# A fused window-attention block and separable convolution, its strips of rows worked one by one or in pairs

## The chip, the cores and the metric

One core of one Trainium2 chip runs the kernel as one program. Its engines are TensorE (PE, matmuls; PEld is its weight load), VectorE (DVE), ScalarE (ACT), GpSimd (POOL) and SyncE (SP), which only issues DMAs here. Each runs its own list of instructions in order, and they meet at semaphores. The metric is device time in microseconds (us).

## The reference, cut to what matters

The input x is (16, 112, 112, 96) in float32. First comes a block of shifted-window attention, then a depthwise 3 x 3 convolution with a pointwise one and a batch norm:

```python
xn = layer_norm(x); xs = roll(xn, (-3, -3)); windows of 7 x 7 tokens
q, k, v = windows @ qkv_w + qkv_b          # 3 heads of 32
attn = softmax(q k^T * scale + bias + mask)  # 49 x 49 per window and head
x1 = x + roll(window_reverse(attn v @ proj_w + proj_b), (3, 3))
y  = x1 + fc2(gelu(fc1(layer_norm(x1))))     # 96 -> 384 -> 96
z  = depthwise_3x3(relu(y)) + dw_bias
out = batch_norm(z @ pw_kernel + pw_bias)
```

## The kernel before, in words

A strip is one row of 16 windows, 7 image rows of 112 pixels. There are 16 of them per image and 256 in all. Everything is float32. Each engine has a function `step(t, phase)` that calls the stages in an order written out by hand, and `steps` calls it for every t with strips at different stages in it: in step t, strip t has its softmax and attention, t+1 its queries, keys and values, t+2 its turn of x, t+3 its first layer norm, t-1 its MLP, t-3 its depthwise convolution and t-4 its pointwise convolution and its store.

The stages, with the engine and the line of their main instruction:

- `scores` (PE, L346) multiplies queries and keys into banks 0 to 2. `add_bias` (DVE, L810) adds the bias table and writes `prob`, `find_max` (DVE, L819) takes the row maxima, `shift` (POOL, L954) subtracts them, `exps` (ACT, L573) takes exponentials, `add_up` (DVE, L826 and L828) sums and takes reciprocals, `divide` (POOL, L963) scales. Each of these is three instructions per strip, one per group of heads. `prob` exists once, so add_bias waits for the turned probabilities of the strip before.
- `turn_probs` (PE, L465) transposes `prob` after `divide`, `probs_turned` (ACT, L635) copies it out, `weigh_values` (PE, L474) multiplies with the values, `attention_out` (ACT, L648 to L653) writes `attnT`, `project` (PE, L535) follows.
- `turn_probs` of groups 0 and 1 uses the banks from which `values` (DVE, L861) copies the next strip's values, so it waits for that copy (`v_ready`).
- `add_x` (DVE, L905, L868 to L883) adds the input and takes the second layer norm's statistics; `root` (POOL, L969, L972) makes scales; `normalise` (ACT, L606) and `rest` (POOL, L980) share the seven columns of tokens, four and three. `turn_x1`, `x1_turned` (PE L411, ACT L616) turn it.
- The MLP is `hidden` (PE, L428), `gelus` (ACT, L627) and `second_layer` (PE, L442 and L446), in two halves. `into_map` (ACT, L682) writes relu of the sum into `ymap`, a ring of areas of rows.
- The depthwise convolution is nine taps over the map, `tap` 0 (DVE, L848) and `tap` 1 to 8 (DVE, L850), each one pass over 7 x 112 pixels. For the strip next to an image's last one each tap is split in two. `pointwise` (PE, L523), `outputs` (ACT, L599) and SP's `store` end a strip.
- The first layer norm is `norm_x` (DVE), `first_scale` and `first_rest` (POOL), `first_norm` (ACT); `turn_x` (PE, L509) and `x_turned` (ACT, L663) turn it; `queries_keys` and `values` follow (PE, L376, L379, L394).
- ACT needs one table for the exponential and another for Gelu. `load_gelu` (L688) and `load_exp` (L692) are one-element activations that bring the load forward. In every strip there is one of each.
- SP issues in each step `move_keys` (part of the keys to other partitions), `store` and `load` of a later strip's input.

The lists that set the order are the calls of `step` at L540 to L557 (PE), L704 to L726 (ACT), L910 to L932 (DVE) and L1002 to L1012 (POOL).

Of the kernel before, what the change touches and what calls it, by code (L numbers as in the profile page):

```python
# [58 lines left out]
AREAS = 6  # L59
TOP_ROWS, LOW_ROWS = 5, 2  # L60

ACT_NORM = HALVES[0][1]
BIAS_LOADS = NT + 1
UNROLL = 4


def swin_conv_kernel(nc, x, qkv_w, qkv_b, proj_w, proj_b, rel_bias_rt, ln1_g, ln1_b, ln2_g, ln2_b,
# [25 lines left out]
    def steps(eng, step, first=-4):  # L93

        for t in range(first, NS + 4):
            step(t, t % UNROLL)
# [13 lines left out]
    with ExitStack() as ctx:  # L110
# [28 lines left out]
        x1 = sb("x1", PT_, 2, WS, C)  # L139
# [76 lines left out]
        def _(sp):  # L216
# [20 lines left out]
            def load(t, phase):  # L237
                s = t + 4
                if not has(s):
                    return  # L240
                slot = phase

                wait(sp, x1_ready, nth(t, 2, 1))
# [8 lines left out]
            def store(t, phase):  # L252
                i = t - 4
                if not has(i):
                    return
                slot = phase % 2

                wait(sp, out_ready, nth(i, 2, 1))
                image, k = i // NWIN, (i + 1) % NWIN
# [6 lines left out]
            def move_keys(t):  # L266
                if not has(t + 1):
                    return
                for u, (a, b) in enumerate(((96, 64), (32, 0))):
                    wait(sp, q_ready, nth(t + 1, 2, u))  # L270
                    sp.dma_start(k0[b:b + HD, :], qk[a:a + HD, u * HALF:(u + 1) * HALF]).then_inc(k0_moved, 16)

            def step(t, phase):
                move_keys(t)
                store(t, phase)
                load(t, phase)

            load(-4, 0)
            load(-3, 1)
            load(-2, 2)  # L280
# [16 lines left out]
            steps(sp, step, first=-1)  # L297
            stores = [(NS + 1) // 2, NS // 2]
            sp.wait_ge(out_stored[1], 32 * stores[0])
            sp.wait_ge(out_stored[0], 32 * stores[1])  # L300
# [3 lines left out]
        def _(pe):  # L304
# [24 lines left out]
            def scores(t):  # L329
                if not has(t):  # L330
                    return
                wait(pe, q_ready, nth(t, 2, 1))
                wait(pe, k_copied, nth(t, 1, 0))
                wait(pe, k0_moved, 32 * (t + 1))
                wait(pe, o_ready, nth(t - 1, 1, 0))
                wait(pe, h_ready, nth(t - 2, 6, 5))
                if t < 2:
                    wait(pe, xt_ready, nth(t + 1, 2, 1))
# [31 lines left out]
            def queries_keys(t):  # L370
                if not has(t + 1):
                    return
# [713 lines left out]
```

## Time and profile before

| | |
|---|---|
| median of 3 runs | 5510.72 us (5488.98 to 5522.0) |
| the profiled execution's own time | 5488.53 us |
| its span, first to last instruction | 5486.8 us |
| PE busy | 5291.6 us (96%) |
| DVE busy | 5129.3 us (93%) |
| ACT busy | 5060.9 us (92%) |
| POOL busy | 3786.2 us (69%) |
| mean granted TensorE clock | 0.993 |
| loads of an ACT table | 255 at L688, 254 at L692, 1283 ns each |

Busy time is the time in which an engine had at least one instruction under way. Matmuls overlap in the engine's pipeline and their ends are modelled, so the distance from the start of one group of matmuls to the start of the next is the better measure of what a group takes. Waits for an own earlier result, on DVE above all, are in no busy sum. The time column of the timeline is us from the span's start.

### The profile page before, as it was taken

The numbers are of one execution on the slowest core, as the hardware profiler recorded it, in microseconds if no ns is written. First come the engines' busy times: TensorE is split into PE (matmuls) and PEld (weight loads), VectorE is DVE, ScalarE is ACT, GpSimd is POOL, SyncE is SP. The second block draws the span as 40 slices with busy tenths as digits, with TensorE's granted clock in tenths as the row PEclk, the third lists the DMA queues.
The fourth block names the chain that finished last, engine by engine and source line by source line (L and its number), as shares of the span: only waits on it lengthen the run. The fifth ranks groups of instructions, "written<-read, shape, count | busy, mean of one in ns | idle before, by whom it ended". The sixth has DMA issues, their size and how long they took to land.

```text
span 5486.8 us, 203158 instructions
## 1 busy us (share of the span) xinstructions
PE 5291.6 (96%) x81186; PEld 3789.4 (69%) x81186; DVE 5129.3 (93%) x13773; ACT 5060.9 (92%) x11038; POOL 3786.2 (69%) x4105
## 2 busy tenths in 40 slices
PE   5999999999999999999999999999999999999998
PEld 3767767676766676767777676767676767677675
DVE  4999999999999999999999999999999999999998
ACT  4999999999999999999999999999999989999996
POOL 3777767777777677777777677777777767777673
PEclk9999999999999999999999999999999999999998
DMA  1111111111111111111111111111111111111110
GB/s 25 34 36 35 36 36 37 35 36 35 36 35 36 35 36 35 36 35 36 36 35 38 36 36 35 36 35 36 36 36 36 37 34 36 36 35 36 37 36 24
DMA packets 275650, 193.70 MB, mean 35 GB/s; under 512 B 229160, under 2 KB 246041, under 8 KB 274713
## 3 DMA queue, kind: packets, MB, share of 16 engines
q1 hardware_dynamic: 274712, 180.70, 12.6%
q8 instruction: 650, 10.65, 0.8%
q14 instruction: 288, 2.35, 0.1%
HBM read 77.81 MB, written 77.07 MB: 28 GB/s over the span
## 4 chain that ended last, share of the span: by engine, by line
PE 57%; DVE 19%; ACT 12%; issue 6%; POOL 4%; SPq 1%; DVEq 0%; DMA 0%; ACTq 0%; POOLq 0%
PE bank L428 19%; PE bank L446 18%; DVE smax L819 7%; DVE prob L810 7%; PE bank L535 6%; PE bank L346 6%; PE bank L474 4%; ACT probT L635 4%; POOL prob L954 3%; ACT xT L663 3%; ACT o_tile L599 3%; PE bank L442 3%; DVE acc L850 2%; ACT prob L573 1%; POOL prob L963 1%
## 5 line engine op out<-in xcount | busy, mean ns | idle before, releaser
L850 DVE SCALAR_TENSOR_TENSOR acc<-ymap,taps,acc 96x784 f32<-96x784 f32 (+2 forms) x2176 | 2137.3, 987 | 54.9
L969 POOL TENSOR_TENSOR rstd<-var_eps,minus_half 112x7 f32<-112x7 f32 x512 | 1114.0, 2176 | 1266.0 <-DVE var_eps L883 1266.0
L428 PE MATMUL bank<-x1T,w 96*128 96x448 f32 (+1 forms) x3072 | 1148.3, 510 | 19.7 <-issue 10.5
L446 PE MATMUL bank<-hT,w 128*96 128x448 f32 (+1 forms) x3072 | 1097.1, 493 | 0.0
L627 ACT ACTIVATE hT<-bank,bfc 128x448 f32<-128x448 f32 (+1 forms) x1536 | 772.6, 564 | 11.9 <-PE bank L428 11.4
L428 PEld LDWEIGHTS bank<-x1T,w 96*128 96x128 f32 x3072 | 542.8, 190 | 346.6 <-issue 204.3
L954 POOL TENSOR_TENSOR prob<-prob,smax 128x392 f32<-128x392 f32 x768 | 653.6, 851 | 159.2 <-DVE smax L819 147.0
L980 POOL TENSOR_SCALAR xn<-x_in,minus_mean,rstd 112x96 f32<-112x96 f32 x768 | 680.9, 897 | 45.2 <-POOL offset L972 45.1
L446 PEld LDWEIGHTS bank<-hT,w 128*96 128x96 f32 x3072 | 466.3, 163 | 342.4 <-issue 165.4
L963 POOL TENSOR_TENSOR prob<-prob,srec 128x392 f32<-128x392 f32 x768 | 632.2, 852 | 81.7 <-DVE srec L828 81.7
L682 ACT ACTIVATE ymap<-bank,cols 96x128 f32<-96x128 f32 (+6 forms) x1056 | 603.2, 679 | 92.4 <-PE bank L446 92.4
L573 ACT ACTIVATE prob<-prob 128x392 f32<-128x392 f32 x768 | 411.6, 536 | 136.5 <-POOL prob L954 117.9
L810 DVE TENSOR_TENSOR prob<-bank,table 128x392 f32<-128x392 f32 x768 | 430.6, 561 | 104.3 <-PE bank L346 104.2
L535 PEld LDWEIGHTS bank<-wproj,attnT 97*112 97x112 f32 x3584 | 396.9, 179 | 102.4 <-issue 100.7
L819 DVE TENSOR_REDUCE smax<-prob 128x8 f32<-128x392 f32 x768 | 430.7, 561 | 26.5
L394 PEld LDWEIGHTS bank<-wv,xT 96*49 96x49 f32 x8192 | 366.4, 125 | 99.6 <-issue 99.6
L523 PE MATMUL bank<-wpw,acc 97*112 97x96 f32 x3584 | 416.4, 268 | 17.2 <-DVE acc L850 16.3
L606 ACT ACTIVATE x1n<-x,offset,rstd 112x96 f32<-112x96 f32 x1024 | 394.2, 456 | 29.6 <-POOL offset L972 10.8
L606 ACT ACTIVATE xn<-x_in,offset,rstd 112x96 f32<-112x96 f32 x1024 | 390.4, 451 | 29.4 <-POOL offset L972 29.4
L663 ACT COPY xT<-bank 96x448 f32<-96x448 f32 (+1 forms) x512 | 400.0, 887 | 16.3 <-PE bank L509 7.0
L376 PE MATMUL bank<-xT,wqk 96*128 96x392 f32 x1024 | 409.6, 523 | 1.1 <-ACT xT L663 1.0
L523 PEld LDWEIGHTS bank<-wpw,acc 97*112 97x112 f32 x3584 | 374.1, 178 | 51.2 <-DVE acc L850 17.0
(100 smaller groups left out, 10286.4 us busy)
## 6 DMA issues: line engine op xcount, KB each, us to landing
out<-o_tile SPq DMA_DIRECT2D x256, 210.0 KB, 2.5
x_in<-in_x SPq DMA_DIRECT2D x256, 168.0 KB, 2.9
x_in<-in_x SPq DMA_DIRECT2D x256, 126.0 KB, 2.9
k<-qk SPq DMA_DIRECT2D x512, 49.0 KB, 1.9
out<-o_tile SPq DMA_DIRECT2D x256, 84.0 KB, 2.5
hT<-in_L_conv_rel_bias SPq DMA_DIRECT2D x49, 0.6 KB
x1T<-in_L_conv_fc_w SPq DMA_DIRECT2D x1, 144.0 KB, 2.6
w<-in_L_conv_fc_w SPq DMA_DIRECT2D x1, 144.0 KB, 2.4
```

Source lines behind the costliest of these rows:

```text
L428: pe.matmul(bank[(1, 2, 5)[m]][:, 0:n * PT_], w1[:, m * 128:(m + 1) * 128], x1T[:, first * PT_:(first + n) * PT_], start=True, stop=True). ...
L446: mm = pe.matmul(bank[b][0:C, 0:n * PT_], w2[:, m, :], hT[:, m, first * PT_:(first + n) * PT_], start=False, stop=(m == MC - 1))
L523: mm = pe.matmul(bank[3 + i][0:HW, a * C:(a + 1) * C], acc[:, phase % 2, first + a, :], wpw[:], start=True, stop=True)
L535: mm = pe.matmul(bank[b][0:PT_, a * C:(a + 1) * C], attnT[:, col * WS:(col + 1) * WS, :], wproj[:], start=True, stop=True)
L606: last = act.activation(dst[:, j], src[:, j], ACT.Identity, bias=b["offset"][:, j:j + 1], scale=b["rstd"][:, j:j + 1])
L627: act.activation(hT[:, m, first * PT_:(first + n) * PT_], bank[(1, 2, 5)[m]][:, 0:n * PT_], ACT.Gelu_apprx_tanh, bias=bfc1[:, m:m + 1]).th ...
L810: dve.tensor_tensor(prob[:, at, 0:NT], bank[g][:, 0:PAIRS * NT].rearrange("p (a m) -> p a m", m=NT), bias[:, at], ALU.add).then_inc(s_bias ...
L819: dve.tensor_reduce(smax[:, at], prob[:, at, 0:NT], AX_X, ALU.max).then_inc(max_ready, 1)
L850: last = dve.scalar_tensor_tensor(out=dst, in0=src, scalar=taps[:, i:i + 1], in1=dst, op0=ALU.mult, op1=ALU.add)
L954: pool.tensor_tensor(p, p, m, ALU.subtract).then_inc(shifted, 1)
L963: pool.tensor_tensor(p, p, r, ALU.mult).then_inc(p_ready, 1)
L969: pool.tensor_tensor(b["rstd"][:], b["var_eps"][:], minus_half[0:PT_], ALU.pow)\
```

## The change

`steps` now goes over pairs of strips, (a, b) = (a, a + 1), and each engine's list is written for a pair. The softmax parts of a and of b come after each other in the first half, the MLPs of a-1 and of a in the second. One `load_exp` and one `load_gelu` stand in a pair's list. The banks of PSUM are chosen by the strip's parity, x1 has three slots, the map has seven areas, and the waits follow the new order. The convolution of a strip may start up to two strips after it and its pointwise part comes five strips after. The old lists, shown above, are left out here, as are edits that only rename or follow the banks.

```diff
-AREAS = 6
+AREAS = 7
...
+SCORE_BANKS = ((0, 1, 2), (0, 5, 3))
+QUERY_BANKS = ((4, 1), (3, 4))
+KEY_BANK = (2, 5)
+VALUE_BANKS = ((0, 5), (6, 7))
+X_BANKS = ((1, 2), (3, 2))
+X1_BANKS = ((1, 6), (0, 5))
+PROB_BANKS = ((6, 7, 3), (0, 5, 4))
+OUT_BANKS = ((4, 6), (1, 6))
+HIDDEN_BANKS = (0, 5, 4)
+SECOND_BANKS = ((7, 6), (3, 2))
...
+    def steps(eng, step):
+
+        for a in range(-4, NS + 6, 2):
+            step(a, a + 1)
...
-            return (4 + image % 2) * AREA
-        return (3 if k == NWIN - 1 else k % 3) * AREA
+            return (5 + image % 2) * AREA
+        return (4 if k == NWIN - 1 else k % 4) * AREA
...
-        x1 = sb("x1", PT_, 2, WS, C)
+        x1 = sb("x1", PT_, 3, WS, C)
...
+            def step(a, b):
+                for t in (a, b):
+                    if t >= 0:
+                        load(t + 3)
+                    if t >= -1:
+                        move_keys(t + 1)
+                        store(t - 5)
...
+            def scores(s):
+                if not has(s):
+                    return
+                wait(pe, q_ready, nth(s, 2, 1))
+                wait(pe, k_copied, nth(s, 1, 0))
+                wait(pe, k0_moved, 32 * (s + 1))
+                if s % 2 == 0:
+                    wait(pe, h_ready, nth(s - 2, 6, 5))
+                    wait(pe, x1t_ready, nth(s - 2, 2, 1))
+                    wait(pe, ymap_ready, nth(s - 3, 2, 1))
+                    if s < 4:
+                        wait(pe, xt_ready, nth(s + 1, 2, 1))
+                        wait(pe, v_ready, nth(s, 2, 1))
+                else:
+                    wait(pe, x1t_ready, nth(s - 2, 2, 1))
+                    wait(pe, pt_ready, nth(s - 1, 3, 2))
+                    if s < 2:
+                        wait(pe, s_biased, nth(s - 1, 3, 2))
+                banks = SCORE_BANKS[s % 2]
...
+            def turn_probs(s, h):
+                if not has(s):
+                    return
+                wait(pe, p_ready, nth(s, 3, h))
                 if h < 2:
+                    wait(pe, v_ready, nth(s + 1, 2, h))
                 else:
+                    wait(pe, out_ready, nth(s - 5, 2, 0))
+                    if not has(s - 5):
+                        wait(pe, q_ready, nth(s + 1, 2, 0))
...
+            def step(a, b):
+                scores(a)
+                queries_keys(b)
+                values(b, 0)
+                values(b, 1)
+                pointwise(a - 5, 0)
+                pointwise(a - 5, 1)
+                turn_x1(a - 1)
+                turn_probs(a, 0)
+                turn_probs(a, 1)
+                turn_probs(a, 2)
+                turn_x(a + 2)
+                weigh_values(a)
+                scores(b)
+                project(a)
+                queries_keys(a + 2)
+                values(a + 2, 0)
+                values(a + 2, 1)
+                pointwise(a - 4, 0)
+                pointwise(a - 4, 1)
+                turn_probs(b, 0)
+                turn_probs(b, 1)
+                turn_probs(b, 2)
+                turn_x(a + 3)
+                weigh_values(b)
+                hidden(a - 1, 0)
+                project(b)
+                hidden(a - 1, 1)
+                second_layer(a - 1, 0)
+                turn_x1(a)
+                second_layer(a - 1, 1)
+                hidden(a, 0)
+                hidden(a, 1)
+                second_layer(a, 0)
+                second_layer(a, 1)
...
+            def step(a, b):
+                into_map(a - 2, 0)
+                into_map(a - 2, 1)
+                load_exp(a)
+                queries(b)
+                exps(a, 0)
+                exps(a, 1)
+                exps(a, 2)
+                keys(b)
+                outputs(a - 5, 0)
+                x1_turned(a - 1)
+                outputs(a - 5, 1)
+                probs_turned(a, 0)
+                probs_turned(a, 1)
+                probs_turned(a, 2)
+                x_turned(a + 2, 0)
+                attention_out(a)
+                x_turned(a + 2, 1)
+                first_norm(a + 3)
+                queries(a + 2)
+                exps(b, 0)
+                exps(b, 1)
+                exps(b, 2)
+                outputs(a - 4, 0)
+                keys(a + 2)
+                outputs(a - 4, 1)
+                probs_turned(b, 0)
+                probs_turned(b, 1)
+                probs_turned(b, 2)
+                x_turned(a + 3, 0)
+                load_gelu(a - 1)
+                attention_out(b)
+                gelus(a - 1, 0)
+                x_turned(a + 3, 1)
+                second_norm(a)
+                gelus(a - 1, 1)
+                x1_turned(a)
+                into_map(a - 1, 0)
+                into_map(a - 1, 1)
+                gelus(a, 0)
+                gelus(a, 1)
+                second_norm(b)
+                first_norm(a + 4)
...
+            def step(a, b):
+                tap(a - 4, 4)
+                add_bias(a, 0)
+                add_bias(a, 1)
+                find_max(a, 0)
+                find_max(a, 1)
+                add_bias(a, 2)
+                find_max(a, 2)
+                add_up(a, 0)
+                values(b, 0)
+                add_up(a, 1)
+                add_up(a, 2)
+                values(b, 1)
+                norm_x(a + 3)
+                tap(a - 4, 5)
+                tap(a - 4, 6)
+                tap(a - 4, 7)
+                tap(a - 4, 8)
+                add_bias(b, 0)
+                find_max(b, 0)
+                add_bias(b, 1)
+                find_max(b, 1)
+                add_bias(b, 2)
+                find_max(b, 2)
+                add_up(b, 0)
+                add_up(b, 1)
+                values(a + 2, 0)
+                add_up(b, 2)
+                values(a + 2, 1)
+                add_x(a)
+                tap(a - 3, 0)
+                tap(a - 3, 1)
+                tap(a - 3, 2)
+                tap(a - 3, 3)
+                tap(a - 3, 4)
+                tap(a - 3, 5)
+                tap(a - 3, 6)
+                add_x(b)
+                tap(a - 3, 7)
+                norm_x(a + 4)
+                tap(a - 3, 8)
+                tap(a - 2, 0)
+                tap(a - 2, 1)
+                tap(a - 2, 2)
+                tap(a - 2, 3)
...
+            def step(a, b):
+                divide(a, 1)
+                divide(a, 2)
+                first_scale(a + 3)
+                first_rest(a + 3)
+                shift(b, 0)
+                shift(b, 1)
+                shift(b, 2)
+                divide(b, 0)
+                divide(b, 1)
+                divide(b, 2)
+                second_scale(a)
+                second_rest(a)
+                second_scale(b)
+                first_scale(a + 4)
+                first_rest(a + 4)
+                second_rest(b)
+                shift(a + 2, 0)
+                shift(a + 2, 1)
+                shift(a + 2, 2)
+                divide(a + 2, 0)
```

## Rows read from the trace of the kernel before

**Rows 1.** Busy time by stretches, sum and mean of eight strips from 2700 us
```profile
sum 166.80, PE 163.39 PEld 116.95 DVE 159.03 ACT 157.69 POOL 117.99; mean PE 20.42 PEld 14.62 DVE 19.88 ACT 19.71 POOL 14.75
```

**Rows 2.** Timeline, PE, one strip: start us, us, engine, line, operation, count, idle before
```profile
2701.25 0.55 PE L509 MATMUL bank<-ident,xn 112*96 112x112 f32 x4
...
2701.92 0.83 PE L411 MATMUL bank<-ident,x1n 112*96 112x112 f32 x7
2702.59 1.46 PE L465 MATMUL bank<-ident,prob 113*113 113x113 f32 x12
2704.41 1.09 PE L474 MATMUL bank<-probT,vw 49*32 49x49 f32 x96 [0.36 <-ACT probT L635]
2705.53 2.52 PE L428 MATMUL bank<-x1T,w 96*128 96x448 f32 x6
2707.89 1.53 PE L535 MATMUL bank<-wproj,attnT 97*112 97x96 f32 x14
2709.28 1.93 PE L428 MATMUL bank<-x1T,w 96*128 96x336 f32 x6
...
2711.43 2.42 PE L446 MATMUL bank<-hT,w 128*96 128x448 f32 x6
2713.69 0.45 PE L442 MATMUL bank<-ident,x 112*96 112x112 f32 x3
...
2715.77 1.30 PE L346 MATMUL bank<-k,qk 32*49 32x49 f32 x96
...
2722.10 0.55 PE L509 MATMUL bank<-ident,xn 112*96 112x112 f32 x4
```

**Rows 3.** Timeline, DVE: first bias, one strip, last bias and last taps
```profile
74.50 0.56 DVE L810 TENSOR_TENSOR prob<-bank,table 128x392 f32<-128x392 f32 x1
...
2696.33 0.57 DVE L810 TENSOR_TENSOR prob<-bank,table 128x392 f32<-128x392 f32 x1 [0.30 <-PE bank L346]
...
2701.93 0.20 DVE L828 RECIPROCAL srec<-ssum 128x8 f32<-128x8 f32 x1
...
2702.48 1.01 DVE L848 TENSOR_SCALAR acc<-ymap,taps 96x784 f32<-96x784 f32 x1
2703.42 1.21 DVE L868 BATCH_NORM_STATS2 stats<-x_in 112x6 f32<-112x96 f32 x7
...
2705.46 5.34 DVE L850 SCALAR_TENSOR_TENSOR acc<-ymap,taps,acc 96x784 f32<-96x784 f32 x5
2710.72 0.91 DVE L905 TENSOR_TENSOR x<-bank,x_in 112x384 f32<-112x384 f32 x2
...
2713.72 3.16 DVE L850 SCALAR_TENSOR_TENSOR acc<-ymap,taps,acc 96x784 f32<-96x784 f32 x3
2717.18 0.57 DVE L810 TENSOR_TENSOR prob<-bank,table 128x392 f32<-128x392 f32 x1 [0.30 <-PE bank L346]
...
5424.25 0.57 DVE L810 TENSOR_TENSOR prob<-bank,table 128x392 f32<-128x392 f32 x1 [1.95 <-PE bank L346]
...
5471.58 8.50 DVE L850 SCALAR_TENSOR_TENSOR acc<-ymap,taps,acc 96x784 f32<-96x784 f32 x8
```

**Rows 4.** Timeline, POOL, the same strip
```profile
2700.88 2.47 POOL L963 TENSOR_TENSOR prob<-prob,srec 128x392 f32<-128x392 f32 x3 [0.32 <-DVE srec L828]
2705.62 2.20 POOL L969 TENSOR_TENSOR rstd<-var_eps,minus_half 112x7 f32<-112x7 f32 x1 [2.27 <-DVE var_eps L883]
...
2708.86 2.64 POOL L980 TENSOR_SCALAR xn<-x_in,minus_mean,rstd 112x96 f32<-112x96 f32 x3 [0.18 <-POOL offset L972]
...
2717.12 1.23 POOL L980 TENSOR_SCALAR x1n<-x,minus_mean,rstd 112x96 f32<-112x96 f32 x3 [0.18 <-POOL offset L972]
```

**Rows 5.** Timeline, ACT, around the Gelu table's load
```profile
2706.87 0.24 ACT L653 COPY attnT<-bank 96x21 f32<-96x21 f32 x1
2707.12 1.28 ACT L688 ACT_TABLE_LOAD   x1
...
2708.53 1.64 ACT L627 ACTIVATE hT<-bank,bfc 128x448 f32<-128x448 f32 x3
```

More of the change, by code:

```diff
@@ L327, in _ @@
             pe.wait_ge(dve_cleared, 2)
-            def scores(t):
-                if not has(t):
+            def scores(s):
+                if not has(s):
                     return
[L332 to L338, printed above, removed]
+                wait(pe, q_ready, nth(s, 2, 1))
[14 more added lines that the diff above has]
+                banks = SCORE_BANKS[s % 2]
                 def score(g, w):
@@ L473, in weigh_one, with weigh_values @@
                 h = HEAD_OF[g][q // 2]
-                return pe.matmul(bank[(4, 0)[odd]][h * HD:(h + 1) * HD, at:at + NT],
-                                 vw[rows, phase % 2, q, side, h * HD:(h + 1) * HD],
+                return pe.matmul(bank[OUT_BANKS[s % 2][odd]][h * HD:(h + 1) * HD, at:at + NT],
+                                 vw[rows, s % 2, q, side, h * HD:(h + 1) * HD],
                                  probT[rows, g, q, 64 * side:64 * side + NT], start=True, stop=True)
-            def weigh_values(t, phase):
-                if not has(t):
+            def weigh_values(s):
+                if not has(s):
@@ L493, in weigh_values, with turn_x @@
+                wait(pe, pt_ready, nth(s, 3, 2))
                 for q, side, odd in tiles:
[L494 to L496 removed]
+                    weigh_one(s, 2, q, side, odd)
+                    weigh_one(s, 2, q + 2, side, odd)
+                    mm = weigh_one(s, 1, q + 2, side, odd)
                 mm.then_inc(o_psum, 1)
[L499 to L500 removed]
+            def turn_x(s):
+                if not has(s):
@@ L510, in turn_x, with pointwise @@
                     mm.then_inc(xt_psum, 1)
-            def pointwise(t, phase, i):
-                if not has(t - 4):
+            def pointwise(s, i):
+                if not has(s):
                     return
@@ L538, in project @@
                     mm.then_inc(proj_psum, 1)
-            def step(t, phase):
-                scores(t)
-                queries_keys(t)
-                values(t, 0)
-                values(t, 1)
-                pointwise(t, phase, 0)
-                pointwise(t, phase, 1)
-                turn_x(t)
-                turn_x1(t)
-                turn_probs(t, 0)
-                turn_probs(t, 1)
-                turn_probs(t, 2)
-                weigh_values(t, phase)
-                hidden(t, 0)
-                project(t)
-                hidden(t, 1)
-                second_layer(t, 0)
-                second_layer(t, 1)
+            def step(a, b):
[33 more added lines that the diff above has]
+                second_layer(a, 1)
             steps(pe, step)
@@ L735, in _ @@
             dve.memset(ones, 1.0).then_inc(dve_set, 1)
[L736 removed]
+            for b in range(8):
                 last = dve.memset(bank[b][:], 0.0)
@@ L799, in build_table, with add_bias @@
                 dve.wait_ge(dve_set, 13)
-            def add_bias(t, phase, g):
-                if not has(t):
+            def add_bias(s, g):
+                if not has(s):
                     return
```

549 lines of the change are left out of this document (249 added, 300 removed).

## The prediction, made before the change was run

> **What bounds the kernel now.** I read busy shares first: over eight strips of steady state the table by stretches gives, of 20.85 us each, TensorE (PE) 20.42, VectorE (DVE) 19.88, ScalarE (ACT) 19.71, GpSimd (POOL) 14.75 [rows 1]. Three engines are nearly full, so shares alone cannot say what ends last. The timeline of one strip can. A strip is 20.85 us: the PE group of L509 starts at 2701.25 and again at 2722.10 [rows 2]. In it PE has one visible gap, 0.36 us before L474, ended by ACT's copy of probT [rows 2]; DVE has one, 0.30 us before L810, ended by the score matmuls L346 [rows 3]. So PE occupies 20.49 us of a strip and DVE 20.55 us, in time from one start to the next. (Busy sums are smaller for DVE, because waits on its own previous result are not in them.) ACT has 1.1 us of slack by the sum. The two sides hand over to each other: scores to bias on DVE, reciprocal to POOL's divide, to PE's turn of the probabilities, to the rest of PE's list, to the next scores.
>
> That hand-over is a loop through two engines that are both full. It costs nothing only while each has other work in front of the wait. So what counts is not how much work a pair of strips has, but how much of it stands in series inside this loop.
>
> **What is removed.** Per pair, two of the four ACT table switches. The end of attnT's last copy (2706.87 + 0.24) to the first Gelu at 2708.53 is 1.42 us [rows 5]. So ACT loses 2.8 us per pair, 360 us over 128 pairs. By itself this is worth at most the two gaps on PE and DVE: if both vanished, the slower one, DVE, would allow 20.55 us per strip, 41.1 per pair.
>
> The Trainium skill ("ScalarE: Activation LUTs", What ACT_TABLE_LOAD costs and Rules for kernel authors) says to do all of one set before switching, and budgets 1283 ns for the load plus about 1380 ns of drain. The 1.28 us of the load agrees with the row; the drain does not show, since 1.42 is the whole switch here. By the page's figure ACT would be given back 5.3 us a pair, but neither amount enters my sum, as ACT does not set the end.
>
> **What is added or only moved.** No compute instruction is added on PE, DVE or POOL: the same calls stand in another order. x1 has three slots, the map seven areas, banks are fixed per parity. On SP, load(a+4) stands ahead of move_keys(a+2) and waits until add_x(a) has ended (about 21 us into the pair, below); the moved keys are wanted at the pair's end, some 20 us later, so this costs 0, and if that cover failed it would cost the DMA alone. Between -0.2 and +0.5 us a pair I leave for it and for PE's transitions between kinds of matmul, whose order changes: the two nearest rows are PE's change from L428 to L535, where six matmuls of 448 columns take 2.36 us up to the next group, and L446, where the same size takes 2.26 (2711.43 to 2713.69): 0.1 a transition [rows 2]. The gap of 0.36 in the same rows makes the upper end. I take 0 for the centre, the order being mixed either way.
>
> **The loop in the new order.** Let T=0 be the start of scores(a) on PE. The terms:
>
> 1. Scores(a) to the first bias: L346 starts 2715.77, L810 at 2717.18 [rows 2, 3]: 1.41.
> 2. DVE's softmax part of a with the two value copies: 2696.33 to 2702.48 [rows 3]: 6.15. Two biases in front of the first maximum move little within it.
> 3. norm_x(a+3): 2703.42 to 2705.46: 2.04.
> 4. Taps 5 to 8 of a-4: five taps take 2705.46 to 2710.72, so 1.052 each: 4.21.
> 5. DVE's softmax part of b up to the end of the last reciprocal: 2696.33 to 2701.93 + 0.20: 5.80.
> 6. POOL's last divide: (2.47 / 3) + start 0.08 = 0.90 [rows 4]; with the hand-over to PE 0.1.
> 7. The third turn of probabilities, a third of 1.46: 0.49 [rows 2].
>
> Terms 1 to 7 give 21.1: from scores(a) to the end of turn_probs(b, 2), all in series on DVE and POOL. PE's own list up to there is shorter: scores to pointwise is 6.33 (2715.77 to 2722.10), twice 12.66, plus turn_x1 and turn_x 0.67 each, turn_probs 1.46 twice, weigh_values 1.12 and project 1.39: 19.4. So PE arrives early and waits 1 to 1.5 us inside turn_probs(b), for divide and for the value copy of a+2.
>
> 8. Then everything that is left on PE stands behind it in order: turn_x 0.67, weigh_values 1.12 (2704.41 to 2705.53), two MLPs, project 1.39 (2707.89 to 2709.28), turn_x1 0.67 (2701.92 to 2702.59). An MLP is 2705.53 to 2715.77 without project: 10.24 - 1.39 = 8.85, twice 17.70. Together 21.55 [rows 2].
>
> Sum 42.65 against 41.70 for two strips before. I know of two further delays. POOL's first_rest(a+3): root to the end of the xn rows is 2705.62 to 2711.50 [rows 4], 6.04 after the end of norm_x, so it ends at 15.6; the first maximum of b is ready at 13.81 (terms 1 to 4) + 1.16 (the bias is 0.57 [rows 3], the maximum about the same) = 14.97, so shift(b, 0) starts 0.6 late, of which DVE's adding-up absorbs half: +0.3. ACT's load_gelu(a-1) stands in front of attention_out(b); counting ACT from turn_x(a+3), o_ready comes at 25.7 where PE wants project(b) at 25.6: +0.1 to +0.2. Full sum 43.2; without them 42.65. I take 43.0.
>
> DVE has 41.1 us of work per pair, so it idles 1.9 us in front of add_bias(a), and PE about as much in turn_probs(b). **What is late next:** where before PE waited 0.36 for ACT and DVE 0.30 for PE per strip, now each of the two waits for the other once a pair, for longer. Moving one more tap from between the two softmax parts to in front of add_bias(a) would shorten the loop by 1.05; the change puts only tap 4 there.
>
> **The sum.** The profiled execution took 5488.53 us with a span of 5486.8, 1.7 around it; that is 0.4% below the median of the three runs (5510.72), and I work from the profiled one. Its first bias starts at 74.50 and its last at 5424.25 [rows 3]: 255 strips at 20.98, so 0.13 over the steady length (split taps of an image's last rows and a few stalls), 0.26 a pair. After: 127 pairs at 43.0 + 0.26 = 5494.0, plus terms 2 to 4 from the bias of 254 to that of 255, 12.4. Tail: before it is 62.5 us (5424.25 to 5486.8). After it DVE has 45 taps left instead of 36 (the convolution trails by up to five strips): 47.3 us, plus the softmax part without its two value copies (6.15 less about 0.95), 5.2, two add_x of 3.00 (2710.72 to 2713.72), 6.7 from the end of the last tap to the end, and about 2.5 of waiting for the last map: 67.7. Total 74.5 + 5494.0 + 12.4 + 67.7 + 1.7 = **5650 us**, 2.9% slower. The likeliest case's own range: a loop of 42.4 (42.65 less 0.25 for transitions) gives 5574, one of 43.7 (43.2 plus 0.5) gives 5739.
>
> **Rivals.**
> A. *Both engines stay full, faster.* If DVE never waits, a pair is 41.1: 127 x 41.36 + 156.3 = 5409, 1.4% faster. Place: turn_probs(b). Condition: the loop is at most 41.1, 1.55 us under my 42.65. For it: ACT's relief is real, and ACT ended PE's only steady wait [rows 2, 5]. Against: ACT is in none of the terms 1 to 5. It decides if taps or MLP groups run shorter than in the rows, which nothing in them shows. The skill's page "Perfetto Trace Analysis" (Identifying the Most-Contended Engine) says not to judge PE by matmul busy time but by weight-load share; here that is PEld 14.62 of 20.85, 70% [rows 1], which would say that PE has room. The rows' start-to-start spacing says it has not: groups follow each other without a gap.
> B. *No change.* The loop comes to 41.7, 5485 +- 25: it needs 1 us of my terms to be hidden. Same rows against it; it is the ground between A and the forecast.
> C. *A further wait inside the loop, much slower.* If ACT, in the order probs_turned(b), x_turned, load_gelu, attention_out(b), gelus, is over 1 us later than I count it, or POOL's second_rest (three rows of 0.41 beside bias and maximum, 0.88 under taps, [rows 4]) delays turn_x1(a), a pair is 44.3 or more: 127 x 1.3 more, 5815. Against it: I count 3 us of room for x1n, and 0.2 short for ACT.
>
> **Chances.** Forecast (5574 to 5739) 70%, C 10%, A 12%, B 8%. Range 5530 to 5750: it takes in the bounds of the unknown transition costs and the upper part of B's side; A and C lie outside. Faster by over 0.5% (what a measurement of this kernel can tell from none) 0.12, within 0.5% 0.08, slower 0.80.
>
> **What would show it.** Right: steady starts of scores(a) 42.4 to 43.7 us apart; the wait of L810 on L346 once a pair, near 2 us; PE's gap in front of L465 of strip b, over 0.5 us, ended by POOL's divide or DVE's value copy; ACT's idle time up by 2.5 us or more a pair; table loads at half their number. Wrong: DVE without a gap in front of add_bias(a) (rival A), or the longest PE wait at L535 or L474 on ACT (rival C), or a DVE share above 96%.

## The result, and the profile after

The changed kernel takes 6191.76 us (median of four runs, 6175.5 to 6246.8) against 5508.85 for the kernel before: a ratio of 1.126 [1.118, 1.134]. The forecast was 5650, at most 5750. Slower was right. The size was not, by 540 us, and the cause of those 540 us stands nowhere in the prediction.

The profiled execution took 6196.48 us. Its page, sections 1 to 3:

```profile
span 6194.7 us, 201917 instructions
PE 5853.5 (94%) x81186; PEld 4207.0 (68%) x81186; DVE 5186.3 (84%) x13776; ACT 4775.2 (77%) x10528; POOL 3820.6 (62%) x4105
PEclk7988898898999888998889988889988899888898
q8 instruction: 647, 10.60, 0.7%
```

In the kernel before, the PEclk line is 9 in all but the last slice; here 25 of the 40 slices show 8 or 7. The granted clock of the whole run is 0.894, before 0.993. So next I laid windows one whole pair of strips long over the run, as [rows 1] did for single strips. The first row is an undisturbed pair (its window starts 2.1 us behind scores(a)), the second a disturbed one:

```profile
2469.00:2511.62 42.62, 41.09 (x636) 29.34 (x635) 39.87 (x107) 37.31 (x83) 29.97 (x32) 1.00 0.14 35
2679.87:2729.88 50.01, 47.47 (x635) 34.27 (x634) 40.47 (x107) 37.35 (x83) 31.30 (x36) 0.86 0.12 30
```

The columns are the stretch and its length, the busy time (and count) of PE, PEld, DVE, ACT and POOL, PEclk, the DMA share and GB/s. The same instructions take 42.62 us or 50.01. DVE, ACT and POOL have nearly the same busy time in both; PE's busy time grows by 6.4 us, and PEclk is 1.00 against 0.86. Over 118 steady pairs, counted from the starts of the score matmuls and the records of the clock: 31 are undisturbed (mean 42.72), 8 have a gap of over 0.5 us in scores(b) and keep the clock (43.41), 75 have the gap and lose the clock (49.93, of which 14.6 us at half clock), and 4 lose the clock without a gap inside scores(b) (48.42). These 4 have a gap of the same kind right beside the group: 2.06 us in front of its first matmul in one, 0.74 to 1.75 us in project behind it in three. All together: 47.54 a pair.

**What a disturbed pair looks like.** PE's timeline (columns as in [rows 2]; L365 is scores, L513 weigh_values, L586 project, L400, L403 and L419 queries, keys and values):

```profile
2738.68 0.55 PE L555 MATMUL bank<-ident,xn 112*96 112x112 f32 x4
...
2739.45 1.10 PE L513 MATMUL bank<-probT,vw 49*32 49x49 f32 x96
2740.49 1.16 PE L365 MATMUL bank<-k,qk 32*49 32x49 f32 x86
2743.76 0.39 PE L365 MATMUL bank<-k,qk 32*49 32x49 f32 x10 [2.11 <-issue]
2744.08 1.62 PE L586 MATMUL bank<-wproj,attnT 97*112 97x96 f32 x14
2745.53 2.58 PE L400 MATMUL bank<-xT,wqk 96*128 96x392 f32 x4
2748.03 1.58 PE L403 MATMUL bank<-xT,wk 96*64 96x392 f32 x4
2749.40 2.77 PE L419 MATMUL bank<-wv,xT 96*49 96x96 f32 x32
```

PE stops within one group of equal matmuls, 86 done and 10 to go, for 2.11 us, and what ended the gap is given as "issue": no semaphore. In the kernel's list no wait stands inside this group. Behind it four matmuls of queries take 2.58 us, in the undisturbed pair 1.51. The clock by stretches around it:

```profile
2730.00:2740.50 10.50, 10.42 (x276) 8.52 (x275) 8.83 (x29) 9.46 (x19) 5.98 (x8) 1.00 0.16 40
2740.50:2743.70 3.20, 1.14 (x90) 1.02 (x87) 3.09 (x3) 3.02 (x10) 2.94 (x3) 1.00 0.02 5
2743.70:2752.00 8.30, 8.24 (x64) 5.57 (x63) 5.59 (x12) 3.06 (x7) 5.31 (x8) 0.63 0.01 2
2752.00:2760.00 8.00, 8.00 (x134) 7.53 (x130) 7.70 (x23) 4.78 (x8) 4.67 (x5) 0.53 0.33 90
2760.00:2774.00 14.00, 14.00 (x63) 8.81 (x63) 11.39 (x39) 11.80 (x31) 6.06 (x5) 1.00 0.08 23
```

The granted clock is full before and in the gap, falls to its lower level (1.2 GHz) behind it although PE is busy again, and is full again in the last stretch.

**The same place undisturbed** shows the loop that the prediction worked out. This pair has a small gap, 0.69 us, in front of scores(b), and is no longer for it than the others, since PE waits at turn_probs(b) anyway. PE first (L504 is turn_probs, L465 hidden):

```profile
2466.91 1.30 PE L365 MATMUL bank<-k,qk 32*49 32x49 f32 x96
...
2478.12 1.29 PE L365 MATMUL bank<-k,qk 32*49 32x49 f32 x96 [0.69 <-issue]
...
2485.82 0.57 PE L504 MATMUL bank<-ident,prob 113*113 113x113 f32 x4
2486.88 1.05 PE L504 MATMUL bank<-ident,prob 113*113 113x113 f32 x8 [0.49 <-DVE vw L949]
2487.77 0.55 PE L555 MATMUL bank<-ident,xn 112*96 112x112 f32 x4
...
2489.57 2.52 PE L465 MATMUL bank<-x1T,w 96*128 96x448 f32 x6
2492.37 1.61 PE L586 MATMUL bank<-wproj,attnT 97*112 97x96 f32 x14 [0.28 <-ACT attnT L733]
...
2509.52 1.30 PE L365 MATMUL bank<-k,qk 32*49 32x49 f32 x96
```

Then DVE in the same pair (columns as in [rows 3]; L899 is the bias, L938 the taps, L949 the copy of the values):

```profile
2468.32 1.04 DVE L899 TENSOR_TENSOR prob<-bank,table 128x392 f32<-128x392 f32 x2 [2.78 <-PE bank L365]
...
2474.31 1.21 DVE L956 BATCH_NORM_STATS2 stats<-x_in 112x6 f32<-112x96 f32 x7
...
2476.35 4.23 DVE L938 SCALAR_TENSOR_TENSOR acc<-ymap,taps,acc 96x784 f32<-96x784 f32 x4
2480.50 0.55 DVE L899 TENSOR_TENSOR prob<-bank,table 128x392 f32<-128x392 f32 x1
...
2486.10 0.20 DVE L917 RECIPROCAL srec<-ssum 128x8 f32<-128x8 f32 x1
2486.22 0.52 DVE L949 COPY vw<-bank 128x384 f32<-128x384 f32 x1
...
2510.93 1.04 DVE L899 TENSOR_TENSOR prob<-bank,table 128x392 f32<-128x392 f32 x2 [1.46 <-PE bank L365]
```

And the waits of the whole run:

```profile
DVE prob L899 <- PE bank L365: 345.6, 200, 9.4
PE bank L365 <- issue: 168.8, 92, 2.3
```

PE's 92 waits in front of or inside scores for "issue" sum to 168.8 us. That is a quarter of the 683 us between the kernels, but the gaps by themselves cost less than their length: a pair with a gap that keeps its clock is 0.69 us longer (43.41 against 42.72), one that loses the clock as well 7.2 us.

### The profile page after: what moved, and what is told of

Same layout as the page of the kernel before. It is cut to its first block, busy times and chain, and to the rows that moved or that the text cites. A ratio compares the mean times of both kernels' runs of the same rounds, so it can differ in the third digit from the quotient of the medians.

```text
span 6194.7 us, 201917 instructions
## 1 busy us (share of the span) xinstructions
PE 5853.5 (94%) x81186; PEld 4207.0 (68%) x81186; DVE 5186.3 (84%) x13776; ACT 4775.2 (77%) x10528; POOL 3820.6 (62%) x4105
## 3 DMA queue, kind: packets, MB, share of 16 engines
q8 instruction: 647, 10.60, 0.7%
q14 instruction: 283, 2.32, 0.1%
## 4 chain that ended last, share of the span: by engine, by line
PE 77%; DVE 10%; issue 6%; ACT 6%; SPq 1%; POOL 0%; DMA 0%; DVEq 0%; ACTq 0%; POOLq 0%
PE bank L487 16%; PE bank L465 13%; PE bank L586 7%; PE bank L400 6%; PE bank L572 6%; PE bank L504 6%; PE bank L419 5%; PE bank L365 5%; PE bank L403 3%; PE bank L483 3%; PE bank L443 2%; PE bank L513 2%; PE bank L555 2%; DVE acc L938 2%; DVE ssum L915 2%
## 5 line engine op out<-in xcount | busy, mean ns | idle before, releaser
L938 DVE SCALAR_TENSOR_TENSOR acc<-ymap,taps,acc 96x784 f32<-96x784 f32 (+2 forms) x2176 | 2157.8, 996 | 59.5
L1078 POOL TENSOR_TENSOR rstd<-var_eps,minus_half 112x7 f32<-112x7 f32 x512 | 1024.5, 2001 | 1419.2 <-DVE var_eps L971 1419.2
L465 PE MATMUL bank<-x1T,w 96*128 96x448 f32 (+1 forms) x3072 | 1095.2, 500 | 1.2 <-ACT x1T L695 0.6
L465 PEld LDWEIGHTS bank<-x1T,w 96*128 96x128 f32 x3072 | 564.5, 190 | 374.2 <-issue 242.6
L899 DVE TENSOR_TENSOR prob<-bank,table 128x392 f32<-128x392 f32 x768 | 419.2, 560 | 346.1 <-PE bank L365 345.6
L915 DVE TENSOR_REDUCE ssum<-prob 128x8 f32<-128x392 f32 x768 | 414.7, 540 | 253.9 <-ACT prob L641 253.8
L1089 POOL TENSOR_SCALAR x1n<-x,minus_mean,rstd 112x96 f32<-112x96 f32 x768 | 597.3, 788 | 22.9 <-POOL offset L1081 22.8
L649 ACT ACTIVATE qk<-bank,bqkv 128x392 f32<-128x392 f32 x512 | 282.4, 575 | 412.3 <-PE bank L400 411.8
L419 PEld LDWEIGHTS bank<-wv,xT 96*49 96x49 f32 x8192 | 471.3, 152 | 139.2 <-issue 137.0
L586 PEld LDWEIGHTS bank<-wproj,attnT 97*112 97x112 f32 x3584 | 458.9, 212 | 155.0 <-ACT attnT L733 137.7
L586 PE MATMUL bank<-wproj,attnT 97*112 97x96 f32 x3584 | 505.3, 304 | 54.7 <-ACT attnT L733 46.1
L365 PE MATMUL bank<-k,qk 32*49 32x49 f32 x24576 | 370.9, 219 | 196.3 <-issue 168.8
L572 PE MATMUL bank<-wpw,acc 97*112 97x96 f32 x3584 | 502.8, 303 | 17.8 <-DVE acc L938 15.4
L504 PE MATMUL bank<-ident,prob 113*113 113x113 f32 x3072 | 490.0, 307 | 30.9 <-DVE vw L949 19.4
L365 PEld LDWEIGHTS bank<-k,qk 32*49 32x49 f32 x24576 | 327.8, 127 | 276.8 <-issue 269.4
```

What stands on the lines that cost most here:

```text
L365: return pe.matmul(bank[banks[g]][64 * side:64 * side + NT, p * NT:(p + 1) * NT], qk[rows, w * NT:(w + 1) * NT], (k0 if HEAD_OF[g][u] == 0 ...
L419: mm = pe.matmul(bank[VALUE_BANKS[s % 2][i]][64 * odd:64 * odd + NT, at:at + C], xT[:, w * NT:(w + 1) * NT], wv[:], start=True, stop=True)
L465: pe.matmul(bank[HIDDEN_BANKS[m]][:, 0:n * PT_], w1[:, m * 128:(m + 1) * 128], x1T[:, first * PT_:(first + n) * PT_], start=True, stop=Tru ...
L504: mm = pe.transpose(bank[PROB_BANKS[s % 2][h]][0:PAIR, q * PAIR:(q + 1) * PAIR], prob_flat[:, (h * PAIRS + 2 * q) * 64:][:, 0:PAIR], ident ...
L572: mm = pe.matmul(bank[QUERY_BANKS[s % 2][i]][0:HW, k * C:(k + 1) * C], acc[:, s % 2, first + k, :], wpw[:], start=True, stop=True)
L586: mm = pe.matmul(bank[b][0:PT_, k * C:(k + 1) * C], attnT[:, col * WS:(col + 1) * WS, :], wproj[:], start=True, stop=True)
```

## The theories

**I, delivery.** PE has run out of instructions. It executes 81186 matmuls, as many weight loads and some 3,370 pure waits, 165.7 thousand in all. The page's queue "instruction" moved 647 packets of 10.60 MB: 64 bytes per instruction, 16 KB a packet, so 256 PE instructions. The Trainium skill ("Runtime: NRT & Kernel Launch", Instruction fetch mechanics) says the same: PE's instruction memory is refilled in blocks of 16 KiB, 256 instructions. It adds that crossing a border is mostly hidden, because an engine dispatches slower than the blocks arrive. The trace contradicts that for this stretch: weigh_values and scores together are 384 instructions of matmuls only 49 columns wide, and up to the gap above 182 pairs of load and matmul ran in 2.2 us (2739.45 to 2741.65), 6 ns an instruction. Beside that gap, the DMA view of 2740.5 to 2741.6 has one such packet:

```profile
GB/s 0 0 0 0 0 0 0 0 0 0 0 0 0 0 0 0 0 0 0 0 0 0 0 0 0 0 0 0 0 0 0 0 0 596 0 0 0 0 0 0
q8 instruction: 1, 0.02, 5.4%
```

It starts in the 34th of 40 slices, 2741.43, just before PE stops, and takes 0.95 us (5.4% of 16 engines in 1.1 us); the next matmul follows 1.4 us after it. Over 82 gaps that last distance is 1.2 to 1.6 us. The kernel before has the same two groups, each alone between groups of long matmuls; the change puts scores(b) directly behind weigh_values(a).

That predicts more: whether a border of 256 falls badly is a matter of counting (**Ia**, the place decides). A pair has 1294 PE instructions, 5 x 256 + 14. The gap should move 14 instructions, 7 matmuls, per pair. It does: from the pair of a = 10 on, the matmuls of scores(b) in front of it number 59, 52, 45, 38, 31, 24, 17, 10, then five pairs have no gap, a sixth has it behind the group, then 89, 82. About every 18 pairs (256/14) there are some five undisturbed ones. Sorted by the place of scores(b) in the count mod 256 (counted from PE's first instruction): at 3 to 173 all pairs have the gap, at 175 to 185 some, at 187 to 243 none inside the group but for one of 0.8 us (two more stand in front of its first matmul, 0.69 us at 193 and 2.06 at 195), and at 245 to 1 none inside it, but six of 0.37 to 1.75 us in project behind it.

The stops themselves say it more sharply. In the traces of all 13 kernels of this document, PE has 636 waits of over 0.5 us that end by "issue" behind the first 80 us. In 626 of them the matmul that PE takes up again is number 193, 194 or 195 of a block of 256, counted from PE's first instruction, whatever stage it belongs to.

**G, clock.** A gap in this place costs the clock, however it arises. The rivals: the wait is one for data or a semaphore that the trace does not name; the clock falls for a reason of its own (the new order of matmuls); or the pairing is slow through the loop of handovers alone.

## The experiments

All compute the whole result unless said otherwise; intervals are of the ratio to the kernel before on the same chip.

**lock_free: a pair of 1280 PE instructions, and 52 small matmuls ahead.** Fourteen waits a pair that another wait already covers are dropped or moved to a matmul that can carry them; with 5 x 256 instructions every pair sees the borders in the same place, and the matmuls in the setup choose it (each is four of PE's instructions): scores(b) at 215 mod 256.
```diff
+            for _ in range(52):
+                pe.matmul(bank[1][:, 0:1], w1_raw[:, 0:128], cols[:, 3:4], start=True, stop=True)
...
-                wait(pe, k0_moved, 32 * (s + 1))
...
-                    wait(pe, h_ready, nth(s - 2, 6, 5))
-                    wait(pe, x1t_ready, nth(s - 2, 2, 1))
...
-                    wait(pe, pt_ready, nth(s - 1, 3, 2))
```


> The changed kernel, its PE list made 14 instructions per pair shorter (waits that an earlier wait of the same list already covers, or that can sit on a neighbouring matmul), so that a pair is 1280 instructions, five times 256, and 52 small matmuls added to the setup so that scores(b) always starts at position 215 of a block of 256. All work is done. Theory I (PE runs out of instructions: the 2 us gap inside scores(b) sits at one position of the 16 KB instruction packets, and TensorE's clock falls after it): no gap, clock 1.0, every pair as the undisturbed ones, 42.7 us, 127 x 42.7 + 156 + 3 = 5580 us. Theory II (the gap is a wait on data or on a bank, or the pair's order is slow in itself): the gap and the clock stay, 6150 to 6200 us.

Measured: 5635.65 us, 1.024 [1.022, 1.025], clock 0.989. No steady pair has the gap; a pair takes 42.82 on the mean. Its row of waits that answers to the 168.8 us above:

```profile
PE bank L362 <- issue: 2.9, 2, 1.6
```

556 us of the loss are gone, with the order of the work on all engines as in the changed kernel. It is 56 us over the expectation. The setup matmuls are part of it: DVE waits 26.4 us for them instead of 4.3, and the first bias starts at 96.58 instead of 74.60. The first two pairs are longer too (48.4 and 49.3 us).

**lock_hit: the same with 36 matmuls, place 151.**
```diff
-            for _ in range(52):
+            for _ in range(36):
```


> As lock_free, but with 36 instead of 52 small matmuls in the setup, so that scores(b) always starts at position 151. 16 small matmuls fewer are 64 instructions. Theory I: the gap of 1.5 to 2.3 us in every pair and the clock at half speed after nearly all of them, 50.3 us per pair, 127 x 50.3 + 160 = 6550 us. Theory II: the same time as lock_free within 0.1%.

Measured: 5624.58, 1.022 [1.020, 1.024], clock 0.996, no gap. A miss. Either Ia is wrong, and fewer waits were the cure, or the edge, some place between 173 and 187 before, has moved.

**few_waits_drift: 11 of the 14 waits removed, no fixed place.** A pair has 1283 instructions, so the place drifts by 3 a pair.
```diff
-                    if i == 0:
-                        wait(pe, x1t_ready, nth(s, 2, 1))
+                    if m == 0:
+                        wait(pe, x1t_ready, nth(s, 2, 1 - half))
```


> lock_hit and lock_free both lost the gap, at two different fixed positions, so the position alone was not it: both also have 14 fewer instructions of PE that only wait. This kernel keeps 11 of these 14 away but has 1283 instructions a pair, and so drifts by 3 a pair through all positions of a 256-instruction block in 85 pairs. Theory Ia (the position decides, and both locks were lucky): gaps in scores(b) come back for a connected part of the positions, up to 70% of the pairs, 5800 to 6150 us. Theory Ib (the waits that stand alone in the list decide, because while PE's queue stands at one the next packet is asked for late): no gaps at any position, 5620 to 5660 us.

Measured: 6139.50, 1.117 [1.113, 1.121]. Few waits are no cure. By place of scores(b): 1 to 134 all with the gap, 137 and 140 a small one, 143 to 149 with it, 152 to 242 none. Ia stands; the edge is near 150 in this list, not near 180, and lock_hit, at 151 in a list with three waits fewer, lies close to it.

How long the 256 instructions before the stopping place had taken bears on this too. Where they had run in under 1.8 us, PE stopped every time: 416 such places in the changed kernel, few_waits_drift, lock_95 and before_weigh_twice, with gaps of 0.8 to 2.6 us. In lock_hit they take 2.3 us, and PE does not stop behind them in 126 of 127 pairs. But this time alone does not draw the edge: in the changed kernel the 17 places with 1.8 to 2.8 us all have a gap (0.31 to 2.33).

**lock_95: 22 matmuls, place 95**, well inside. Against lock_free only 30 of the small matmuls of the setup are left out.
```diff
-            for _ in range(52):
+            for _ in range(22):
```


> lock_free and lock_hit again, now with scores(b) fixed at position 95 of the 256-instruction block. In few_waits_drift, whose list differs by three waits, all positions from 1 to 134 had the gap in scores(b) and 152 to 242 had none: 151 in lock_hit was at the edge, since the waits that were taken out stood in front of it. The list is that of lock_free but for 30 small matmuls in the setup. Theory Ia (the position decides): a gap in every pair, 49.2 us on the mean of that run's disturbed pairs, 127 x 49.2 + 160 = 6410 us. Theory Ib (the waits that stand alone decide): 5630 us.

Measured: 6328.68, 1.150 [1.148, 1.152], clock 0.879. The gap is in 118 of 118 steady pairs, always between the same two matmuls, 49 before and 47 behind it; 108 pairs lose the clock with it (49.03 us), 10 don't (43.61). PE in one of them:

```profile
2722.47 1.10 PE L505 MATMUL bank<-probT,vw 49*32 49x49 f32 x96
2723.50 0.73 PE L362 MATMUL bank<-k,qk 32*49 32x49 f32 x49
2725.94 0.93 PE L362 MATMUL bank<-k,qk 32*49 32x49 f32 x47 [1.71 <-issue]
```

The clock lines of the two pages, lock_free's first:

```profile
PEclk8999999999999999999999999999999999999998
```
```profile
PEclk9898888888988898889888888888899898888988
```

693 us between two kernels that differ in 30 matmuls before the loop begins. No wait for data, no order of matmuls and no handover differs; the place does.

**before_weigh_twice: the kernel before, with weigh_values issued twice** (192 short matmuls in a row, the second 96 writing the same values again).
```diff
-                for q, side, odd in tiles:
...
+                for again in range(3):
+                    for q, side, odd in tiles:
+                        if again == 1:
+                            weigh_one(phase, 0, q, side, odd)
```


> The kernel before with each strip's weigh_values issued twice (the same products into the same banks), so that 192 short matmuls, 384 instructions, stand in a row, as weigh_values(a) and scores(b) do in the changed kernel. The matmuls alone add 1.12 us a strip: 5507 + 287 = 5795 us. Theory I (a run of short matmuls outpaces the delivery of instructions): gaps near 2 us inside or behind the second half and stretches of TensorE clock at half, 6000 to 6700 us. Theory II (it is the pair's order or its banks): 5770 to 5820 us at clock 0.99.

Measured: 6873.08, 1.249 [1.245, 1.253], clock 0.874; the added matmuls by their own time would give about 5795 (256 strips x 1.12 us more), and the expectation's upper end was 6700. One strip's PE rows:

```profile
2724.25 1.63 PE L474 MATMUL bank<-probT,vw 49*32 49x49 f32 x157 [0.34 <-ACT probT L641]
2728.10 0.73 PE L474 MATMUL bank<-probT,vw 49*32 49x49 f32 x35 [2.22 <-issue]
```

No pairs, other tables, other engines' orders: the same gap. Only the run of short matmuls is common to both. Of 234 steady strips, 67 without the gap take 21.7 us, 34 with the gap alone 23.7, and 133 with gap and low clock 29.5.

**gap_by_wait: lock_free, with a wait put four matmuls into the group scores(b)** (the expectation says two), for attention_out(a), which ends 1.4 us later. It gives PE a gap that has nothing to do with delivery.
```diff
+                    if w == 0 and s % 2:
+                        wait(pe, o_ready, nth(s - 1, 1, 0))
```


> lock_free with a gap of PE made by data in place of missing instructions: scores(b) also waits, two matmuls in, for attention_out(a), which I count 1.6 to 1.8 us later. Of this gap PE's own slack in front of turn_probs(b) takes up 1.2 us. Theory G (any such gap of PE costs the clock): TensorE at half speed after most of these gaps, 49 us per pair, 6300 to 6500 us. Theory H (the clock falls only with missing instructions, or with the short matmuls around them): clock 0.98 or more, 5640 to 5720 us.

Measured: 6378.38, 1.160 [1.155, 1.164], clock 0.870. All 118 pairs have the gap, 1.43 us on the mean, and all lose the clock: 48.82 us a pair against 42.82.

```profile
2738.68 0.29 PE L362 MATMUL bank<-k,qk 32*49 32x49 f32 x4
2740.34 1.27 PE L362 MATMUL bank<-k,qk 32*49 32x49 f32 x92 [1.37 <-ACT attnT L728]
```

So G holds: a semaphore's gap of 1.4 us there costs 6.0 us a pair, at most 1.4 of it the gap itself. lock_free's own wait for the same data, of about 0.45 us in front of project, is in its 42.82 already.

**turnx_between: the changed kernel, with turn_x(a+2) between the two groups.**
```diff
-                turn_x(a + 2)
                 weigh_values(a)
+                turn_x(a + 2)
                 scores(b)
...
-                x_turned(a + 2, 0)
                 attention_out(a)
+                x_turned(a + 2, 0)
```
The second part, on ACT, lets attention_out(a) follow weigh_values(a) directly again; what it is worth alone was not run here.


> The changed kernel with its own instruction counts; only turn_x(a+2) is moved behind weigh_values(a), so that its seven transposes stand between the two runs of 96 matmuls, and attention_out(a) is moved ahead of x_turned(a+2, 0) on ACT. Theory I: 256 instructions last 0.67 us longer there, the gaps shrink from 1.9 to about 1.2 us and fewer pairs lose their clock: 5750 to 6000 us. Theory II: 6190 us or more, since nothing that the scores wait for comes earlier.

Measured: 6015.21, 1.093 [1.088, 1.097], 15 us above the expected range. A partial cure: with seven wider matmuls (0.8 us) between them, the gaps are 1.24 us on the mean instead of 1.85, and 53 pairs of 118 have gap and low clock instead of 75; 31 have a gap and keep the clock instead of 8.

**before_one_table: the kernel before with Exp in place of Gelu** (another function, so another result), and no table switch left. It measures what the change was after.
```diff
-                                   ACT.Gelu_apprx_tanh, bias=bfc1[:, m:m + 1]).then_inc(h_ready, 1)
+                                   ACT.Exp, bias=bfc1[:, m:m + 1]).then_inc(h_ready, 1)
...
-                    act.activation(table_load[:, 1:2], table_load[:, 0:1], ACT.Gelu_apprx_tanh)
+                    act.activation(table_load[:, 1:2], table_load[:, 0:1], ACT.Exp)
```


> The kernel before with Exp in place of Gelu in the MLP, so that ACT never changes its table: the change's first aim by itself, in the old order. It computes another function there. ACT loses 2.6 us of its 19.8 a strip. My prediction says this is worth at most the two gaps of 0.36 and 0.30 us a strip: 5430 to 5507 us. Rival (ACT sets the strip): 2 us or more a strip, under 5000 us.

Measured: 5476.32, 0.995 [0.994, 0.997]. All 509 table loads of the kernel before are worth half a per cent.

**lock_free_tap: lock_free, with tap 5 in front of add_bias(a).** The prediction said that this shortens the loop by 1.05.
```diff
                 tap(a - 4, 4)
+                tap(a - 4, 5)
                 add_bias(a, 0)
```


> lock_free with tap 5 of strip a-4 moved from between the softmax parts of a and b to in front of add_bias(a). My loop of the prediction (DVE from the bias of a to the last reciprocal of b, then all of PE behind it) loses one tap, 1.05 us: the pair falls from 42.6 to 41.6, unless PE's own list takes over: I count that at 41.9. Time 5580 - 127 x 0.7 = 5490 us at 41.9, 5450 at 41.6. Rival (PE or ACT alone sets the pair, DVE's order does not matter): 5580 us, as lock_free.

Measured: 5555.31, 1.009 [1.008, 1.011]. A pair falls from 42.71 to 42.16 (medians), half of the 1.05; 41.6 to 41.9 was expected. PE had only its wait in turn_probs(b) to give, 0.53 us a pair; over the run it falls from 75.0 us to 25.3. What is left is PE's own list with its waits for attnT in front of project, and those are as long as before: 103.5 us in lock_free, 103.9 here. One of them:

```profile
2692.07 1.62 PE L579 MATMUL bank<-wproj,attnT 97*112 97x96 f32 x14 [0.45 <-ACT attnT L726]
```

**free_tap_act: the same, with both attention_out calls one step earlier in ACT's order.**
```diff
-                x_turned(a + 2, 0)
                 attention_out(a)
+                x_turned(a + 2, 0)
...
-                load_gelu(a - 1)
                 attention_out(b)
+                load_gelu(a - 1)
```


> lock_free_tap with two swaps in ACT's list: attention_out(a) ahead of x_turned(a+2, 0), attention_out(b) ahead of load_gelu(a-1). In lock_free_tap PE waited 0.8 us a project for attnT (209 us in all), which is what keeps the pair at 42.15 and not at 41.6. If PE's list sets the pair now: 41.5 or less, 5555 - 127 x 0.65 = 5470 us, a little under the kernel before. Rival (DVE and the hand-over set it): 5555 us.

Measured: 5517.37, 1.002 [1.001, 1.003]; 41.80 a pair (median). The waits for attnT fall to 57.3 us, and the time by 38 us where 85 were expected. The best version in pairs, and no faster than the kernel before.

**free_2taps_act: tap 6 moved as well.**
```diff
                 tap(a - 4, 5)
+                tap(a - 4, 6)
                 add_bias(a, 0)
```


> free_tap_act with tap 6 moved ahead of add_bias(a) as well. If the loop through DVE still sets the pair (41.8 us undisturbed), it comes down to DVE's own 41.1 plus small waits: 41.3, 5517 - 127 x 0.5 = 5455 us, 1% under the kernel before. If PE's list with its waits for ACT sets it: 5517 us, and no order of DVE's taps helps.

Measured: 5648.43, 1.026 [1.024, 1.029], 42.8 a pair. A miss: one tap too many. PE now waits once a pair at a place where it waited 16 times in all in free_tap_act (126 times here, 104.6 us against 6.3):

```profile
2694.27 0.59 PE L437 MATMUL bank<-ident,x1n 112*96 112x112 f32 x4 [0.73 <-ACT k L650]
```

In the timeline ACT's three exponentials of a stand in front of this copy, each behind a wait for POOL's shift, and the copy ends when turn_x1 goes on. So the later softmax of a delays ACT's exponentials, those the copy of the keys, and that turn_x1: the loop then closes through ACT. None of the versions in pairs beats the kernel before.

## Why the prediction was wrong

**Step by step, the loop was right.** From the undisturbed pair above, predicted and measured: term 1 1.41 and 1.41 (2466.91 to 2468.32); term 2 6.15 and 5.99 (to 2474.31); term 3 2.04 and 2.04; term 4 4.21 and 4.15 (to 2480.50); term 5 5.80 and 5.80 (to 2486.30). Terms 6 and 7, priced at 1.49, came to 1.47 (turn_x follows at 2487.77): PE's visible gap there was ended by DVE's value copy (to 2486.74), one of the two that the prediction had named. It is 0.49 long, not the 1 to 1.5 that the prediction expected: PE's own list up to there, priced at 19.4 with the turns of b, takes 20.4 in this pair, 0.69 of it the small stop. Step 8, PE's rest, took 21.75 instead of 21.55. Sum 42.61 against 42.65. ACT idles 5.3 us in this pair (42.62 - 37.31), before 2.3 in two strips [rows 1]. Of the two further delays the one on POOL did not show, and that on ACT did, as 0.28 in front of project(b), and is in the 21.75. The 43.0 that I took was 0.4 too much, DVE's wait in front of add_bias(a) 1.46 instead of 2.

**The step that failed** is in the part on what is added or only moved: "Between -0.2 and +0.5 us a pair I leave for it and for PE's transitions between kinds of matmul, whose order changes", and "I take 0 for the centre". It measured +4.8 (47.54 - 42.72). I had bounded a new neighbourhood by the price of two transitions between groups of long matmuls. The transition that the change creates, weigh_values(a) to scores(b), two groups of short ones, stood in no row of before, and I did not list it. Neither did I treat PE's supply of instructions or its clock as a resource; both lay outside the sum. The trace of before had the sign, though not in the rows that I took: behind weigh_values, in front of hidden, PE has 8 waits of 0.54 to 2.32 us for "issue", 9.9 us in all, each at the same place 193 of a block.

```profile
1778.52 1.09 PE L474 MATMUL bank<-probT,vw 49*32 49x49 f32 x96 [0.34 <-ACT probT L635]
1781.64 3.75 PE L428 MATMUL bank<-x1T,w 96*128 96x448 f32 x6 [2.03 <-issue]
```

Behind this one and behind the one of 2.32 us the granted clock was 0.50 for 10.2 us. The change made a rare event a regular one. In numbers: 127 pairs by 4.8 are 610 us. With pairs of 42.72, the start, fill and tail as they were (74.6 + 10.7 + 73.9 + 1.8), the changed kernel would take 5586 us; lock_free, 5636 with its 22 us later start, bears that out to 28 us. The forecast without the gap would have been 64 us too high: 0.54 a pair too much, and 5 too little at the two ends.

**The rivals.** None of A, B, C was it. A (both engines full, faster) fell where the prediction said, at the loop: even undisturbed, DVE waits once a pair. C was nearest in time and wrong in place: it put the loss on a late ACT or POOL. DVE does wait longer for ACT in the changed kernel (253.8 us for the exponentials, 151.2 for x1n), but in lock_free, without the stops, only 8.5 and 12.2, so these waits follow from them. That ACT's relief is worth little was right: 0.5%, where the two gaps had set 1.4% as the bound.

**Shown and not shown.** Shown: the gap depends on the place of the instructions in the count mod 256 (lock_95 against lock_free, the drift, the one stopping place in all traces), it follows a long run of short matmuls in another kernel too, and a gap of that size there costs the clock nearly always, whatever makes it. Argued from the packets' times, not shown by an edit: that the missing thing is the next block of 16 KB. Open: what triggers a block's request; why removing waits moved the edge from about 180 to about 150; what makes the 8 stops of the kernel before, whose 256 instructions had taken 4.4 us and more; why 8 of 83 pairs with a gap kept the clock in the changed kernel. Whether a gap of this size costs the clock behind other kinds of work than short matmuls was not tried.

## What to carry to other kernels

When a change sets two groups next to each other that were apart, list the new neighbours on each engine, and count instructions as well as microseconds: several hundred loads and matmuls of a few ns each, back to back, can bring PE to a stop, most likely because they outrun their own delivery. A gap ended by "issue" in the middle of equal matmuls is the sign; then look at the granted clock behind it, which can cost several times the gap. And a saving on an engine that ends no wait of size is worth at most the waits that it ends: try it alone first (here 0.5%), before reordering everything for it.

## What the runs showed of the hardware

A gap of 1.2 to 2.3 us on a PE that was busy before and after it brought the granted clock down to 1.2 GHz, mostly for 10 to 17 us, in 75 of 83 pairs of the changed kernel, in 108 of 118 in lock_95 and in 118 of 118 in gap_by_wait; gap and clock together cost 7.2, 6.3 and 6.0 us a pair. 626 of 636 waits of PE for "issue" over 0.5 us stood at one place of the count mod 256. 30 small matmuls in the setup moved the time by 12%. A second identical group of 96 short matmuls, which by its own time adds 1.1 to 1.2 us, cost 5.35 us a strip.
